# Row maxima from two neighbouring PSUM banks with one VectorE instruction, and a ring that hands out one or two banks

## What is computed

```
x = x + tanh(g_xattn) * (softmax(q k^T / 8) v Wo + bo)   # q = layernorm(x) Wq, k = ctx Wk, v = ctx Wv
x = x + tanh(g_ffn) * fp4_linear(silu(gate) * up, w_down) # gate, up = fp4_linear(layernorm(x), w_gate), (.., w_up)
```

## Time and profile before

| what | value |
|---|---|
| median of 3 runs | 597.64 us (597.33 to 598.23) |
| the profiled execution | 598.33 us, its span 596.1 us |
| mean granted TensorE clock | 0.958 of full speed |
| busy share of the span | PE 91%, PEld 56%, DVE 80%, ACT 52%, POOL 46% |
| DMA | 9.31 MB, 16 GB/s on average |

### The profile page before, as it was taken

One profiled execution on the slowest core, in us unless ns is written; L12 is line 12 of the kernel. 1 busy time (PEld: TensorE's weight loads), 2 busy tenths in 40 slices (PEclk: granted clock), 3 DMA queues, 4 the chain that ended last, 5 costly groups with the idle time before them and its releaser, 6 DMA issues.

```text
span 596.1 us, 9833 instructions
## 1 busy us (share of the span) xinstructions
PE 543.8 (91%) x2841; PEld 335.7 (56%) x2841; DVE 476.7 (80%) x793; ACT 312.3 (52%) x723; POOL 276.3 (46%) x234
## 2 busy tenths in 40 slices
PE   5889999999999998999999998999999999999642
PEld 4655565666566554666466554665566565656331
DVE  2769875889977996889977995789977997787655
ACT  3434756575456645575456644566456745546211
POOL 4007344553828173553828173363827264456400
PEclk9779999999999999999999999999999999999675
DMA  8500000200020000200020000200020000000000
GB/s 158 99 1 1 1 1 0 52 2 1 1 58 2 0 2 9 50 0 0 1 56 1 0 0 9 50 0 0 1 56 1 0 0 5 1 1 1 1 3 3
DMA packets 27892, 9.31 MB, mean 16 GB/s; under 512 B 24016, under 2 KB 27600, under 8 KB 27856
## 3 DMA queue, kind: packets, MB, share of 16 engines
q1 hardware_dynamic: 27856, 8.92, 7.5%
HBM read 8.50 MB, written 0.41 MB: 15 GB/s over the span
## 4 chain that ended last, share of the span: by engine, by line
PE 59%; DVE 27%; issue 10%; ACT 2%; DMA 1%; DVEq 0%; POOL 0%; SPq 0%; POOLq 0%; ACTq 0%
PE attn L789 16%; PE scores L775 11%; PE ring L728 10%; DVE max L897 8%; PE scores L776 7%; PE ring L735 4%; PE ring L742 4%; DVE f_abs L362 3%; DVE f_abs L364 2%; DVE e_gate L860 2%; DVE acc_v L919 2%; PE ring L707 2%; DVE h_fp L366 1%; DVE z L871 1%; DVE rsum L904 1%
## 5 line engine op out<-in xcount | busy, mean ns | idle before, releaser
L634 ACT ACTIVATE probs<-scores 120x400 f32<-120x400 f32 (+1 forms) x384 | 190.0, 504 | 211.7 <-PE scores L776 209.1
L897 DVE TENSOR_REDUCE max<-ring 116x1 f32<-116x482 f32 (+1 forms) x336 | 204.7, 649 | 28.4 <-PE ring L728 24.1
L505 POOL TENSOR_TENSOR acc_p<-acc_p,probs 120x800 f32<-120x800 f32 x79 | 156.3, 1978 | 61.7 <-ACT probs L634 58.1
L789 PE MATMUL attn<-probs,ctx_n 120*64 120x400 f32 (+1 forms) x768 | 173.9, 532 | 0.0
L775 PE MATMUL scores<-q_hh,k_hl 128*120 128x400 f32 (+1 forms) x384 | 155.0, 404 | 1.2 <-DVE q_ls L899 1.2
L775 PEld LDWEIGHTS scores<-q_hh,k_hl 128*120 128x120 f32 (+1 forms) x384 | 70.9, 185 | 128.2 <-ACT probs L634 70.2
L776 PE MATMUL scores<-q_ls,k_h 71*120 71x400 f32 (+1 forms) x384 | 134.8, 351 | 0.0
L728 PE MATMUL ring<-k_hl,q_hh 128*116 128x482 f32 (+1 forms) x336 | 119.6, 409 | 12.4 <-DVE max L897 4.7
L776 PEld LDWEIGHTS scores<-q_ls,k_h 71*120 71x120 f32 (+1 forms) x384 | 71.6, 186 | 4.2
L728 PEld LDWEIGHTS ring<-k_hl,q_hh 128*116 128x116 f32 (+1 forms) x336 | 59.1, 182 | 25.7 <-DVE max L897 9.9
L789 PEld LDWEIGHTS attn<-probs,ctx_n 120*64 120x64 f32 (+1 forms) x768 | 38.3, 136 | 46.4 <-issue 34.3
(11 more groups left out here) (127 smaller groups left out, 526.9 us busy)
## 6 DMA issues: line engine op xcount, KB each, us to landing
ctx_n<-in_ctx SPq DMA_DIRECT2D x16, 360.0 KB
wq<-in_L_xattn_Wq SPq DMA_DIRECT2D x1, 512.0 KB, 4.6
wo<-in_L_xattn_Wo SPq DMA_DIRECT2D x1, 512.0 KB, 6.8
x_in<-in_x SPq DMA_DIRECT2D x8, 50.0 KB
out<-y_out SPq DMA_DIRECT2D x8, 50.0 KB
wk<-in_L_xattn_Wk SPq DMA_DIRECT2D x1, 256.0 KB, 4.1
ctx_n<-in_ctx SPq DMA_DIRECT2D x16, 1.0 KB
wv<-in_L_xattn_Wv SPq DMA_DIRECT2D x1, 256.0 KB, 6.3
```

The lines of the kernel that those rows point to most:

```text
L505: pool.tensor_tensor(acc_p[0:r, t.g % 2, :], left, probs[0:r, c % PROBS, :], ALU.add).then_inc(sum_p, 1)
L634: act.activation(probs[0:r, c % PROBS, k * HALF:(k + 1) * HALF], scores[0:r, slot % SCORE_BANKS, 0:HALF], ACT.Exp).then_inc(probs_full, 1)
L789: mm = pe.matmul(attn[64 * i:64 * i + C, k, 0:HALF], ctx_n[0:r, par, c, 0, :], probs[0:r, c % PROBS, k * HALF:(k + 1) * HALF], start=(j == ...
L897: dve.tensor_reduce(max3[0:rows, tile, part:part + 1], src[0:rows, 0:MAXC[part + 1] - MAXC[part]], AX.X, ALU.max).then_inc(free, 1)
```

## The change

A `max` key now names its first unit and how many units it covers, one or two. PE fills two neighbouring banks of the ring with two matmuls, and one DVE reduction reads both and writes two columns of `max3`. The 21 units of a group become ten pairs and one single. The single is the first key of even groups and the seventh of odd groups. To make all units alike, a tile is 115 rows (7 tiles cover 805 rows, the last 5 of them zero) and each part is 482 columns (the last two parts overlap by 2 columns).

The ring counts places. A pair must not run over the end of the four banks, so that a place is skipped where it would. Each use has one semaphore, that of its last bank, and PE waits for every use that last held one of the banks it takes. The tables of slots are rewritten: the maxima stand in other slots, in odd groups from slot 2 on, `gate` and `up` stand together in slot 4, `sum` and the first `proj` together in slot 6, the two `hT` together in slot 19, and the three `ctx` in slots 10, 14 and 15.

```diff
-TILES, TROWS = 7, 116
-TSIZE = [min(TROWS, ROWS - t * TROWS) for t in range(TILES)]
-MAXC = [0, 482, 964, M]
+TILES, TROWS = 7, 115
+PARTS, PCOLS = 3, 482
+PSTART = [0, PCOLS, M - PCOLS]
...
-MAX_SLOTS = {1: 1, 2: 1, 4: 1, 5: 2, 7: 3, 8: 2, 10: 2, 11: 2, 12: 1, 13: 2, 14: 1, 15: 1, 16: 1, 17: 1}
-FFN_SLOTS = {2: ('zT', 0), 4: ('gate', 0), 6: ('up', 0), 19: ('hT', 0), 20: ('hT', 1), 22: ('down', 0)}
-W_SLOTS = {slot: ("wT", i) for i, slot in enumerate(FFN_SLOTS)}
-POST_SLOTS = {6: ('sum', 0), 8: ('proj', 0), 10: ('proj', 1)}
-CTX_SLOTS = {14: ('ctx', 0), 15: ('ctx', 1), 18: ('ctx', 2)}
+MAX_SLOTS = [{1: 1, 2: 1, 4: 1, 5: 1, 7: 1, 8: 1, 9: 1, 11: 1, 12: 1, 13: 1, 16: 1},
+             {2: 1, 3: 1, 5: 1, 7: 1, 8: 1, 9: 1, 10: 1, 11: 1, 12: 1, 14: 1, 16: 1}]
+SINGLE = [0, 6]
+FFN_SLOTS = {1: [('zT', 0)], 4: [('gate', 0), ('up', 0)], 19: [('hT', 0), ('hT', 1)], 22: [('down', 0)]}
+W_SLOTS = {1: [("wT", 0)], 4: [("wT", 1), ("wT", 2)], 19: [("wT", 3), ("wT", 4)], 22: [("wT", 5)]}
+POST_SLOTS = {6: [('sum', 0), ('proj', 0)], 10: [('proj', 1)]}
+CTX_SLOTS = {10: ('ctx', 0), 14: ('ctx', 1), 15: ('ctx', 2)}
...
+def max_units(parity):
+
+    first = [0]
+    for i in range((PARTS * TILES + 1) // 2):
+        first.append(first[-1] + (1 if i == SINGLE[parity] else 2))
+    return [("max", u, v - u) for u, v in zip(first, first[1:])]
...
-BETWEEN = {1: ('ctx', 2), 4: ('wqT', 1), 7: ('A', 1), 9: ('wvT', 0), 13: ('vo', 0), 14: ('vo', 1), 16: ('vo', 2), 20: ('vo', 3)}
-for _u in range(3 * TILES):
-    START += ([BETWEEN[_u]] if _u in BETWEEN else []) + [("max", _u)]
+BETWEEN = {1: [('ctx', 2)], 2: [('wqT', 1)], 4: [('A', 1)], 5: [('wvT', 0)], 7: [('vo', 0), ('vo', 1)], 9: [('vo', 2), ('vo', 3)]}
+for _i, _key in enumerate(max_units(0)):
+    START += BETWEEN.get(_i, []) + [_key]
...
-    index, n = {}, 0
+
+
+    index, place = {}, 0
+    released, last = [0] * RING_BANKS, [None] * RING_BANKS
+
+    def put(g, key):
+        nonlocal place
+        wide = key[2] if key[0] == "max" else 1
+        if place % RING_BANKS + wide > RING_BANKS:
+            place += 1
+        bank = place % RING_BANKS
+        own = bank + wide - 1
+        released[own] += 1
+        before = {}
+        for b in range(bank, bank + wide):
+            if last[b] is not None:
+                before[last[b][0]] = max(last[b][1], before.get(last[b][0], 0))
+            last[b] = (own, released[own])
+        index[(g, key)] = Use(bank, own, released[own], before)
+        place += wide
...
-                if t.g > 0 or n > 1:
-                    pe.wait_ge(ring_free[bank], n - 1)
+                kind, k = key[0:2]
+                bank, own, _ = t.ring(key)
+                for sem_of, n in t.ring_before(key):
+                    pe.wait_ge(ring_free[sem_of], n)
...
-                    rows, a, b = TSIZE[tile], MAXC[part], MAXC[part + 1]
-                    mm = pe.matmul(dst[0:rows, 0:b - a], q_hh[:, (t.g + 1) % 2, tile * TROWS:tile * TROWS + rows], k_hl[par][:, a:b], start=True, stop=True)
+                    for i in range(key[2]):
+                        row, a = (k + i) // PARTS * TROWS, PSTART[(k + i) % PARTS]
+                        mm = pe.matmul(ring[0:TROWS, bank + i, 0:PCOLS], q_hh[:, (t.g + 1) % 2, row:row + TROWS], k_hl[par][:, a:a + PCOLS], start=True, stop=True)
...
-                mm.then_inc(ring_full[bank], 1)
+                mm.then_inc(ring_full[own], 1)
...
-                    tile, part = k // 3, k % 3
-                    rows = TSIZE[tile]
-                    dve.tensor_reduce(max3[0:rows, tile, part:part + 1], src[0:rows, 0:MAXC[part + 1] - MAXC[part]], AX.X, ALU.max).then_inc(free, 1)
+                    parts = max3[0:TROWS, :, :].rearrange("p t k -> p (t k)")
+                    dve.tensor_reduce(parts[:, k:k + key[2]], ring[0:TROWS, bank:bank + key[2], 0:PCOLS], AX.X, ALU.max).then_inc(free, 1)
...
-                wait_reads(dve, (t, ("max", 19)), (t, ("max", 20)))
+                wait_reads(dve, *[(t, key) for key in max_units(0 if t.g < 0 else t.g % 2)])
```

103 lines of the change are left out of this document (55 added, 48 removed).

## The result

The changed kernel takes **650.01 us** (median of 4 runs, 639.65 to 651.89), the kernel before on the same chip 597.93 (median of 4, 597.33 to 599.35). That is 52 us slower, where 12 were predicted.

What follows compares the result with a forecast made beforehand. Odd groups were taken to hang on both PE and DVE, even ones on PE nearly throughout. Even groups' 7.0 us and odd groups' 7.2 made 14.2, taken as 12: 609.6 us against the median, range for 8 in 10 593 to 617.

Steps and rivals of the forecast that it cites:

- The reduction: DVE's maxima: a pair takes 1.15 us, saving 0.07 each; 160 pairs take 11 us from DVE.
- the signs: What the profile would show, among it DVE's busy time down by 20 us and yet no gain.
- The wait of `gate`: Odd groups, slot 4: PE waits 1.4 us until the pair of slot 2 has been read.
- What is late next: Odd groups, after gate: DVE idles for 1.9 us before the pair of slot 5.
- The stretch to the end of `h_fp`: Odd groups, DVE from the sigmoid on: 20.57 us before, 19.93 after, by pairs and row sums there in time.
- +1.2 us for an odd group: hT at 498.6 instead of 497.37 in the group walked; 0.6 to 1.6, six groups, 7.2 us.
- +1.0 us for an even group: Waits before the pairs of slots 4 and 5, `sum` and slot 12; 0.4 to 1.4, seven groups, 7.0 us.
- The two terms at full clock: The losses forecast per group, 1.2 us for an odd one and 1.0 us for an even one.
- the plain sum: Seven even groups, 7.0 us, plus six odd groups, 7.2 us: 14.2 us, of which 12 were taken.
- the clock falls too: Rival: the new 1.4 us gap brings PE to half clock, 10 us more in six odd groups, 619; chance 0.10.
- The rivals of the other sign: DVE's relief reaches hT whole, about 591 us, chance 0.20; the waits only move, 597.6 us, chance 0.08.
- Two banks read apart: Rival: a pair costs two singles or more, 0.15 to 0.22 us more a link, 621 us; chance 0.04.

Runs made afterwards that it cites:

- e7b: Changed kernel's tile size, equal parts and ring code, but single maxima and all slot tables of the kernel before; 601.47 us, ratio 1.004.
- e11: Changed kernel with single units and the maxima back in the slots of the kernel before, single users in the new slots; 604.92 us, ratio 1.013.
- e3: Changed kernel with its slots, tile size and ring, but every maximum a unit of its own; 633.47 us, ratio 1.058.
- e4: Changed kernel with pairs handled jointly, but two reductions in place of the fused one; 654.31 us, ratio 1.097.
- e6b: Changed kernel's pairs, tile sizes and ring, every single user back in its old slot, pairs placed near the old maxima; 660.8 us, ratio 1.101.
- e1: Changed kernel plus eight discarded max matmuls on PE before the wait for the rounded hidden row, odd groups 3 to 13; 629.19 us, ratio 1.052.
- e2: Changed kernel with gate and up in slot 3 ahead of the first pair and odd-group maxima slots adjusted; 627.44 us, ratio 1.046.
- e12: All slot tables of the kernel before, four pairs and thirteen single maxima in each group; 625.11 us.
- e18: Kernel before with one maximum of slot 7 moved to the empty slot 9; 623.37 us, ratio 1.036.
- e13: Single units in the slots where pairs were placed with all single users in their old slots; 641.45 us, ratio 1.072.

## Why the prediction was wrong

A ladder from the kernel before to the changed one, each step a difference of two medians above, with the step by the ratios in brackets: tile size and ring code 3.5 us (2; 597.9 to 601.5, e7b); single users moved 3.5 (5.5; 604.9, e11); maxima in the new slots, still single, 28.5 (27; 633.5, e3); two banks held as one 21 (23; 654.3, e4); the fused instruction -4 (-12; 650.0). Only the third and the fourth are clear of the spread of the runs in size. The steps depend on their order: in the old slots the pairs cost more (e6b), and moving the single users then gives some of it back.

**The reduction.** Right: a pair takes 1.15 us as walked (1.16 at 299.51), the group fell from 204.7 us to 192.0, which is 12.7 where 11 was said. DVE's whole busy time fell by 10.2, where the signs named 20. The kernel got slower all the same; e4 puts the worth of the fused instruction at 4 to 12 us.

**The wait of `gate`.** Right: 1.4 us predicted, 1.55 measured, in six odd groups, behind the pair of slot 2.

**What is late next.** The walk gave 1.9 us of idle DVE before the pair of slot 5. Where `gate` runs at full clock the trace has 2.26 (222.95), near it; in four groups of six it has 3.9, because `gate` and `up` at 2 x 0.59 and attention at 0.82 were priced at full clock, and the wait of 1.55 us just ahead had brought half clock.

**The stretch to the end of `h_fp`.** Predicted 19.93 us, measured 321.21 - 300.59 = 20.6, and 20.6 in the group at 220 us too. The walk carried durations over from the earlier trace rows as if they were constants, and took 0.64 us off. Of the instructions in it `rsum` became 1.55 us shorter, and `acc_v` 0.87 and `f_t` 1.06 longer, since `rsum` now starts when POOL's addition is over and the other two while one runs. And DVE waits 0.69 us for a pair at 304.00, where its waits for maxima in this stretch came to 0.18 before.

**+1.2 us for an odd group.** As a lateness it was near. From `gate` to `hT` the walk had 24.2 us, the group at 220 us took 25.1, and the one before 24.8 (472.56 to 497.37). But the walk followed DVE to `h_fp` and never PE to `hT`. PE came there 23.75 us after `gate` before (497.37 - 1.06 - 472.56), and 22.4 us after it now (244.78 - 2.69 - 219.67), so that its wait grew from 1.06 to 2.69 us, much more than `h_fp` was late. No term of the sum has the length of this wait. Half clock followed it in all six odd groups: attention at 1.60 twice instead of 0.89, scores and `down` in proportion, about 3 us. With what follows the waits of `gate`, this is 15 to 21 us of the kernel by e1.

**+1.0 us for an even group.** Its waits are there, 0.43 us before a pair at 335.18, 0.17 before `sum` at 338.47 and 0.31 before a pair at 349.60, and they sum to about what was said. But from the row sums of the odd group at 299.7 to those of the even one at 338.5 there are 38.8 us, where there were 33.4 before. In e1, where the clock stays up, the same stretch is 35.7 (294.70 to 330.37). So 3.1 of the 5.4 us are the low clock that the odd group's wait at `hT` left behind, for which the sum had no term.

**The two terms at full clock.** e1 shows what the change costs with the clock up: from `hT` to `hT`, an even and an odd group together take 70.4 us (316.31 to 386.70), and 66.25 before (295.08 to 361.33). That is 4.1 us, where the sum had 1.0 + 1.2 = 2.2. Between `gate` and `hT` it is 0.25 (25.07 against 24.82), for which the walk had 0.6 less instead of more. Between `hT` and the next `gate` it is 3.9, for which the walks had 1.0 and 474.4 - 472.56 = 1.8. Which step of the walks missed these last 1.1 us was not found.

**The steps that failed.** Two failed, and they share the loss of 46 to 52 us about so: 15 to 21 us are the clock, and some 31 us the plain sum, which had 14.

The first is the rival *the clock falls too*: "by the rows these gaps are just short of it". It was right in its mechanism and got 0.10, because 1.61 us without a matmul at 236.13 had not brought the low clock and 1.89 at 370.76 had the earlier trace rows. I read two rows as a threshold. Counted over the groups of several traces it is otherwise: half clock followed none of the six waits of 1.06 to 1.12 us at `hT` in the kernel before, four of six of 1.55 at `gate` in the changed kernel and none of six in e1, five of six of 1.6 in e2 and two of six in e12, four of six of 2.1 in e18, and all of 2.7 to 3.05 in the changed kernel, in e3 and in e13. And I applied the rival to the wait of `gate` alone, not to the one at `hT`. Its price of 10 us lacked that second place.

The second is the size of the two terms, 2.2 us for two groups where 4.1 were measured at full clock. Of the 1.9 us missing, 0.8 lie in the stretch in which DVE's durations were taken as constants, and 1.1 where the cause stays open. The walk also took it as free that the maxima stand in other slots: e3, single units in the new slots, is 27 to 28.5 us slower than e11, its lower clock included. Why these slots cost so much is shown in part only. The waits at `gate` and for `h_fp` grow, and the meetings of DVE and POOL shift, as they do in e18 with 21 to 25 us. But e7b shows that the time lost in such meetings does not by itself set the time of the kernel.

The range ended at 617 because of both. That the kernel got slower was forecast for a reason that holds: the waits that were walked are there.

**The rivals of the other sign** (0.28 together): DVE was relieved of 12.7 us of reductions and PE waited for it more. *Two banks read apart* is excluded by the 1.16 us of a pair.

## What to carry to other kernels

When a change shifts the order of work on an engine that shares a path with another (here DVE's SBUF operations and POOL's), re-walk which of the two starts first at every meeting: durations taken from the profile before hold only for the old order, and a shift of a few tenths can be worth 1.5 us. When it makes another engine late or PE early, work out how long PE will wait at every wait on the way, not at the new one alone, and price what runs behind each wait at both clocks. Do not read one wait that kept the clock and one that lost it as a threshold: count all waits of that length in the trace. Before moving a tuned table to make room for a new kind of unit, move it alone: one run with single units in the new slots (e3) would have shown 35 of the 52 us without any pair.
